# One Trainium2 core, expert blocks of a mixture-of-experts stage: which operand of the gate and up products is stationary

## The reference

```python
x = _layernorm(x + _L0_attn_ref(x, ...))   # latent attention, 16 heads
x = _layernorm(x + _L0_ffn_ref(x, gate_w, gate_up_proj, down_proj))
x = _layernorm(x + _L1_attn_ref(x, ...))   # 16 heads, 4 key groups
x = _layernorm(x + _L1_ffn_ref(x, weight, bias))
```

```python
gu = jnp.einsum('th,ehf->etf', x, gate_up_proj)     # h = 256, f = 2 * 128
gate, up = jnp.split(gu, 2, axis=-1)
inter = jax.nn.silu(gate) * up
y = jnp.einsum('eti,eih->eth', inter, down_proj)
out = jnp.einsum('eth,te->th', y, combine)          # combine: 0 but for 2 experts
```

## Time and profile before

| | |
|---|---|
| median of 3 executions | 537.47 us (536.35 to 539.25) |
| the profiled execution | 537.99 us |
| its span in the profile | 535.8 us |
| PE busy | 501.2 us |
| DVE, ACT, POOL busy | 377.3, 338.9, 294.7 us |
| expert stage, first turn_block to last POOL scatter | 225.6 to 281.3 us of the span |

### The profile page before, as it was taken

How to read it: one execution, slowest core, us unless ns; L and a number is a source line. 1 busy time by engine, 2 the same in 40 slices (tenths; PEclk the granted TensorE clock), 3 DMA queues, 4 the chain that set the end, 5 groups by cost and what they waited for, 6 DMA issues and landing times.

```text
span 535.8 us, 10729 instructions
## 1 busy us (share of the span) xinstructions
PE 501.2 (94%) x3600; PEld 437.3 (82%) x3600; DVE 377.3 (70%) x825; ACT 338.9 (63%) x755; POOL 294.7 (55%) x291
## 2 busy tenths in 40 slices
PE   7989999999999998799975879999999999999995
PEld 6768888888888787588854778999999999999884
DVE  2589888888885356755555788779766986678656
ACT  4457777777776655444432588778766876686673
POOL 4746777677775226336560577677544665465330
PEclk8999999999999999799996989999999999999999
DMA  8917999970000292345575000000000000000001
GB/s 265 393 64 281 323 314 329 332 252 0 0 0 1 94 410 79 105 132 160 166 256 187 1 1 2 0 1 2 1 1 2 0 1 2 1 2 1 1 21 60
DMA packets 17613, 56.79 MB, mean 106 GB/s; under 512 B 2612, under 2 KB 12346, under 8 KB 15770
## 3 DMA queue, kind: packets, MB, share of 16 engines
q1 hardware_dynamic: 14816, 49.81, 27.1%
q0 software_dynamic: 2752, 6.40, 3.6%
HBM read 49.19 MB, written 28.45 MB: 145 GB/s over the span
## 4 chain that ended last, share of the span: by engine, by line
PE 77%; DVE 8%; ACT 5%; issue 4%; POOL 3%; DMA 3%; SPq 0%; DVEq 0%; POOLq 0%; ACTq 0%
PE bank L442 10%; PE bank L444 10%; PE bank L443 10%; PE bank L990 5%; PE bank L585 5%; PE bank L507 5%; PE bank L610 3%; PE bank L587 2%; PE bank L734 2%; PE bank L1007 2%; PE bank L719 2%; PE bank L721 2%; PE bank L720 2%; PE bank L621 2%; PE bank L701 2%
## 5 line engine op out<-in xcount | busy, mean ns | idle before, releaser
L1099 ACT ACTIVATE probs<-bank,neg_max,q_scale 128x256 f32<-128x256 f32 (+1 forms) x128 | 63.8, 508 | 38.4 <-DVE neg_max L1742 38.4
L1951 POOL TENSOR_TENSOR probs<-probs,inv_sum 128x512 f32<-128x512 f32 x64 | 51.6, 828 | 44.3 <-DVE inv_sum L1750 44.3
L1984 POOL TENSOR_TENSOR exps<-exps,tables 128x256 f32<-128x256 f32 x32 | 24.6, 769 | 71.8 <-ACT exps L1209 71.7
L1209 ACT ACTIVATE exps<-bank 128x768 f32<-128x768 f32 x32 | 25.9, 809 | 41.3 <-PE bank L701 41.3
L1971 POOL TENSOR_TENSOR swapped<-swapped,tables 128x512 f32<-128x512 f32 x32 | 43.1, 1350 | 10.0 <-ACT swapped L1130 9.8
L1565 DVE TENSOR_TENSOR q_lo<-q_sum,q_hi 128x512 fp32r<-128x512 f32 x32 | 27.2, 851 | 29.7 <-ACT q_hi L1163 29.5
L2084 POOL DMA_INDIRECT y_rows<-y_slot,dest x31 | 29.7, 959 | 29.9 <-issue 19.1
L1728 DVE TENSOR_TENSOR swapped<-bank,tables 32x512 f32<-32x512 f32 x64 | 44.4, 694 | 1.4
L1943 POOL TENSOR_TENSOR qT<-qT,swapped 128x512 f32<-128x512 f32 x32 | 40.8, 1276 | 7.1 <-DVE swapped L1728 7.1
L442 PE MATMUL bank<-x,wq_hi 128*128 128x256 f32 x128 | 38.5, 301 | 3.2 <-DVE q_sum L1552 3.2
L585 PE MATMUL bank<-keysT,qT 128*128 128x256 f32 x128 | 38.3, 381 | 0.0
(11 more groups left out here) (283 smaller groups left out, 1774.2 us busy)
## 6 DMA issues: line engine op xcount, KB each, us to landing
slots<-in_c_unused SPq DMA_DIRECT2D x20, 1036.0 KB, 36.4
gu_all<-in_gate_up SPq DMA_DIRECT2D x4, 1024.0 KB, 7.9
xg<-slots SPq DMA_DIRECT2D x31, 129.5 KB
wvo_raw<-in_wvo SPq DMA_DIRECT2D x1, 2560.0 KB, 20.8
dn_all<-in_down SPq DMA_DIRECT2D x1, 2048.0 KB, 7.7
wq_full<-in_Wq SPq DMA_DIRECT2D x1, 2048.0 KB
wo_raw<-in_Wo SPq DMA_DIRECT2D x1, 2048.0 KB
wqk_raw<-in_wqk SPq DMA_DIRECT2D x1, 1536.0 KB, 10.4
```

The source lines that it names most:

```text
L1099: ins = act.activation(probs[:, par, h, c0:c1], bank[:, 2 * par + h, c0:c1], ACT.Exp, bias=neg_max[:, par, i:i + 1], scale=q_scale[:, b, t ...
L1951: ins = pool.tensor_tensor(some, some, inv, ALU.mult)
```

## The change

In `up` the weights become the stationary operand and the turned rows the moving one: four matmuls of 128 columns in place of two of 256, for gate and up apart. Their results have the 128 features of gate and up on partitions and the tokens along the free axis, which is the form that `down` needs, so DVE's product goes to `actT` directly; `turn_act`, `copy_act` and their PSUM banks are gone, and `down` follows `up` one step later instead of two. PE addresses a fixed place: a new ACT step, `take_weights(k)`, reads the expert's number with a `value_load` on ACT, waits for `up(k-2)` and copies the 512 columns of gate and up weights of block k to one of two buffers in `q_sum`. It stands behind `silu(k-2)` in ACT's order; the first two stand ahead of `copy_block(0)`. PE keeps its own `value_load`, for `down`. `up` has one wait more, on `gu_copied`.

```diff
--- before.py
+++ after.py
@@ -39,6 +39,7 @@
 W = D + 3
 KINDS = 8
 XG = 6
+GU = 2
 YS = 6
 WARM = (20, 42, 18, 14)
 ROUTE = 3 * E + PER_STEP + NB + NT
@@ -272,7 +273,8 @@
     eps, minus_half = table_probe[:, 19:20], table_probe[:, 17:19]
     idx_f = x_rows[:, :, D:D + TOP]
     xT_f32 = q_sum
-    gated, act_tok = (swapped[:, i, 0:2 * FF].rearrange("p (i n) -> p i n", i=2) for i in range(2))
+    gu_block = q_sum[:].rearrange("p g (c f) -> p g c f", c=KD)
+    gated = swapped[:, 0, 0:2 * P].rearrange("p (i n) -> p i n", i=2)
     wk_hi, wk_lo = w_hi, w_lo
     slots = nc.dram_tensor("slots", (REGIONS * REGION, W), F32, kind="Internal").ap()
     y_rows = nc.dram_tensor("y_rows", (TOP * (B * T + KINDS * REGION), D), F32, kind="Internal").ap()
@@ -299,7 +301,7 @@
 
     mo = sems("moe", "xT_copied region_ready row_ids logits_done sigmoid_done marked prefix_done slots_ready "
               "table_sums table_steps "
-              "xgT_done xgT_copied up_done silu_done act_ready actT_done actT_copied down_done y_copied dest_ready")
+              "xgT_done xgT_copied gu_copied up_done silu_done act_ready down_done y_copied dest_ready")
 
     kv = sems("kv1", "kv_hi kv_lo w_hi wq_lo w_lo k_done swap_done cos_done sin_done k_summed "
               "k_hi k_lo v_done v_copied ones")
@@ -378,9 +380,6 @@
 
     def up_bank(k):
         return 2 + k % 2
-
-    def actT_bank(k):
-        return 4 + k % 2
 
     def down_bank(k):
         return 6 + k % 2
@@ -980,26 +979,22 @@
                 mm = pe.transpose(bank[:, turned(k), c * P:c * P + P], xg[:, k % XG, c * P:c * P + P], ident[:])
             mm.then_inc(mo["xgT_done"], 1)
 
-        def up(k, experts):
+        def up(k):
             pe.wait_ge(mo["xgT_copied"], k + 1)
+            pe.wait_ge(mo["gu_copied"], k + 1)
             if k >= 2:
                 pe.wait_ge(mo["act_ready"], k - 1)
-            for c in range(KD):
-                for i, e in enumerate(experts):
-                    rows = slice(ROWS * i, ROWS * i + ROWS)
-                    mm = pe.matmul(bank[rows, up_bank(k), 0:2 * FF], xgT[:, k % 2, c, rows],
-                                   gu_all[:, bass.ds(e, 1), c, :].rearrange("p e f -> p (e f)"),
-                                   start=c == 0, stop=c == KD - 1, skip_group_check=True)
+            for i in range(PER_STEP):
+                rows = slice(ROWS * i, ROWS * i + ROWS)
+                for half in range(2):
+                    dst = bank[:, up_bank(k), half * P + ROWS * i:half * P + ROWS * i + ROWS]
+                    for c in range(KD):
+                        mm = pe.matmul(dst, gu_block[:, k % GU, c, half * FF:half * FF + FF], xgT[:, k % 2, c, rows], start=c == 0, stop=c == KD - 1,
+                                       skip_group_check=True)
             mm.then_inc(mo["up_done"], 1)
 
-        def turn_act(k):
+        def down(k, experts):
             pe.wait_ge(mo["act_ready"], k + 1)
-            if k >= 2:
-                pe.wait_ge(mo["actT_copied"], k - 1)
-            pe.transpose(bank[:, actT_bank(k), 0:P], act_tok[:, k % 2, :], ident[:]).then_inc(mo["actT_done"], 1)
-
-        def down(k, experts):
-            pe.wait_ge(mo["actT_copied"], k + 1)
             if k >= 2:
                 pe.wait_ge(mo["y_copied"], k - 1)
             for i, e in enumerate(experts):
@@ -1015,18 +1010,16 @@
             pe.wait_ge(x_or_expert_in[j], 32)
         turn_block(0)
         experts_of = {}
-        for i in range(STEPS + 2):
+        for i in range(STEPS + 1):
             if i < STEPS:
                 experts_of[i] = [pe.value_load(block_expert[0:1, m:m + 1], min_val=0, max_val=E - 1)
                                  for m in range(PER_STEP * i, PER_STEP * i + PER_STEP)]
             if i + 1 < STEPS:
                 turn_block(i + 1)
             if i < STEPS:
-                up(i, experts_of[i])
-            if 1 <= i <= STEPS:
-                turn_act(i - 1)
-            if i >= 2:
-                down(i - 2, experts_of.pop(i - 2))
+                up(i)
+            if i >= 1:
+                down(i - 1, experts_of.pop(i - 1))
 
         pe.wait_ge(mo["y_copied"], STEPS)
         pe.wait_ge(y_back[0], 16)
@@ -1341,21 +1334,35 @@
             act.activation(xgT[:, k % 2, :, :], bank[:, turned(k), 0:D].rearrange("p (c n) -> p c n", c=KD),
                            ACT.Copy).then_inc(mo["xgT_copied"], 1)
 
+        def take_weights(k):
+            e = act.value_load(block_expert[0:1, k:k + 1], min_val=0, max_val=E - 1)
+            if k >= GU:
+                act.wait_ge(mo["up_done"], k - GU + 1)
+            act.activation(gu_block[:, k % GU, :, :], gu_all[:, bass.ds(e, 1), :, :].rearrange("p e c f -> p (e c) f"),
+                           ACT.Copy).then_inc(mo["gu_copied"], 1)
+
         def silu(k):
             act.wait_ge(mo["up_done"], k + 1)
             if k >= 2:
                 act.wait_ge(mo["act_ready"], k - 1)
-            act.activation(gated[:, k % 2, :], bank[:, up_bank(k), 0:FF], ACT.Silu).then_inc(mo["silu_done"], 1)
+            act.activation(gated[:, k % 2, :], bank[:, up_bank(k), 0:P], ACT.Silu).then_inc(mo["silu_done"], 1)
 
         act.wait_ge(ld["wq1_in"], 16)
         act.wait_ge(ln["y_done"], NT)
         for i in range(PAIRS):
             act.activation(chunk(wq_hi, i), chunk(wq_full, i), ACT.Copy).then_inc(kv["w_hi"], 1)
+        act.wait_ge(mo["table_steps"], 4)
+        for j in range(4):
+            act.wait_ge(x_or_expert_in[j], 32)
+        take_weights(0)
+        take_weights(1)
         copy_block(0)
         for k in range(STEPS):
             if k + 1 < STEPS:
                 copy_block(k + 1)
             silu(k)
+            if k + 2 < STEPS:
+                take_weights(k + 2)
         load_table(act, 2 * B + 8, ACT.Sqrt)
         act_layer1(act)
 
@@ -1902,15 +1909,9 @@
         def gate_block(k):
             dve.wait_ge(mo["silu_done"], k + 1)
             if k >= 2:
-                dve.wait_ge(mo["actT_done"], k - 1)
-            dve.tensor_tensor(act_tok[:, k % 2, :], gated[:, k % 2, :], bank[:, up_bank(k), FF:2 * FF],
+                dve.wait_ge(mo["down_done"], k - 1)
+            dve.tensor_tensor(actT[:, k % 2, :], gated[:, k % 2, :], bank[:, up_bank(k), P:2 * P],
                               ALU.mult).then_inc(mo["act_ready"], 1)
-
-        def copy_act(k):
-            dve.wait_ge(mo["actT_done"], k + 1)
-            if k >= 2:
-                dve.wait_ge(mo["down_done"], k - 1)
-            dve.tensor_copy(actT[:, k % 2, :], bank[:, actT_bank(k), 0:P]).then_inc(mo["actT_copied"], 1)
 
         def copy_y(k):
             dve.wait_ge(mo["down_done"], k + 1)
@@ -1924,14 +1925,12 @@
                                      in1=xg[:, k % XG, D + 2:D + 3], op0=ALU.not_equal,
                                      op1=ALU.add).then_inc(mo["dest_ready"], 1)
 
-        for i in range(STEPS + 2):
-            if 1 <= i <= STEPS:
-                copy_act(i - 1)
+        for i in range(STEPS + 1):
             if i < STEPS:
                 gate_block(i)
                 find_rows(i)
-            if i >= 2:
-                copy_y(i - 2)
+            if i >= 1:
+                copy_y(i - 1)
         dve_layer1(dve, counted, n_step)
```

## The result

The changed kernel takes 534.68 us (median of 15 executions, 533.00 to 537.19), the kernel before, run beside it 15 times, 538.04 (536.28 to 543.22). The ratio is 0.9938 with a 95% interval from 0.9919 to 0.9958: 3.4 us less. The forecast was 534.2 us, with a range from 532.4 to 537.3.

The account below looks back on a forecast made before the run. The prediction took PE, busy throughout the expert stage, as the bound. Terms of -2.0, +0.1 and -1.4 gave -3.3 us: 534.7 from the profiled 537.99, and 534.2 for the median, 0.5 lower; range 532.4 to 537.3.

Parts of the forecast that it names:

- PE's step: Expert stage, PE's work per block: falls from 1.62 to 1.55 us, over 28 steps 2.0 us less.
- the rival with unhidden loads: PE in up: weight loads not hidden behind the products, step 2.41 us, 558 us in all; chance 0.02.
- ACT: Expert stage, ACT's added register load (0.7 us) and weights copy (0.52): hidden, with 1.1 us of work in a 1.55 us step.
- rival (a): ACT's register load takes 1.0 to 1.1 us, silu 0.2 to 0.3 late, step 1.60 to 1.63: 535.6 to 536.1; chance 0.24.
- the margin of 0.03 us: ACT's slack per step: silu can start 1.52 us after the previous silu's start and is due at 1.55.
- PE's register load: PE's expert-number load, now behind down: over at U+1.77, hidden with 0.2 us of cover, costed at nothing.
- U+1.97: Due time of the turn_block queued behind PE's expert-number load, 1.97 us after the end U of an up.
- The head: Pipeline fill at the expert stage's start: 0.1 us more, since down(0) now stands ahead of PE's expert-number load.
- rival (c): Granted clock: a stage ending 3 us sooner can gain or lose a low-clock stretch, up to 1.4 us; no separate chance.
- The margin of 1.4 us: Allowance on both sides of the forecast for a low-clock stretch gained or lost; forecast with it 532.6 to 535.8, chance 0.58.
- The end: Last up's end to last scatter's start: from 4.55 to 3.17 us, 1.38 less, with the last two scatters queued on POOL.
- The sum: Whole kernel: -2.0 + 0.1 - 1.4 = -3.3 us against the profiled execution of 537.99.

## Why the prediction was right

**PE's step.** Right to 0.01 us. up took 0.89 to 0.90, the step 1.546, and 28 of them gave -2.1 us where -2.0 stood. The price came from products of 129 columns with a new weight load each; the eight loads of up are hidden in the same way, and the rival with unhidden loads, 558 us, did not come. The Trainium skill ("TensorE: Matmul & The Clock Gate", Part 3, "What overlaps and what doesn't") asks for another row group for that; eight full-height loads and eight products in 0.90 us disagree with it.

**ACT.** Right, with less room than it looks. Silu to weights was 0.67 us (241.15 to 241.82), taken as 0.7; silu came 0.20 after up's end, as written; copy_block ended 1.76 us after it, where 1.80 stood. Silu follows copy_block without a gap, so the margin of 0.03 us that the sum left was about right. The run with two loads shows rival (a)'s side, the run with the weights copied once shows that nothing of it is paid in the changed kernel. That silu is late only by what exceeds the margin held where a load was added; that the pipeline can go uneven, with PE's ends reaching the others 1 to 2 us late, was in none of the cases. Here there was luck: the changed kernel happened to run in the even way, while two kernels with the same work on each engine, run on another chip, took 542.5 and 544.3, outside the range.

**PE's register load.** Right: turn_block came at 242.93, 1.98 us after up's end and without idle time, where U+1.97 stood; without the load the step is unchanged.

**The head.** Mis-sized: +0.1 stood there, +1.2 was measured in the profiled execution. It is rival (c)'s mechanism, a low-clock stretch in another place than before, not the new wait. The margin of 1.4 us that it had been given held it. In the medians, -3.4, this loss does not show.

**The end.** The last scatter began 3.29 us after the last up, not 3.17 (-1.3 for -1.4), and it is held by POOL's queue as said: the scatter before it went at 276.99 with 0.40 of issue, the last at 278.26, 1.27 later. The kernel with copies alone has 4.36 from the last silu, as before, and so has the turned product with down two steps behind (4.36, and 4.54 with even steps): the gain comes from down following up one step sooner, which the turned product allows.

**The sum.** -3.3 stood there. The profiled pair gives -2.7: 1.1 lost in the head, 0.4 gained outside the span, which had no term. The medians give -3.4.

## What to carry to other kernels

The transpose between two products was had for nothing here by exchanging which operand is stationary; price it by the records of a like product with a new load each, not by the number of loads. When a step is full on two engines, judge it by its steps one by one and not by their mean alone: uneven steps say that something else than the sum of work sets the time. When such a state exists, compare kernels only beside each other on one chip, and put one that is known to be even among them. Before moving a register load on ACT, look for the instruction ahead of it that still waits for a semaphore: the load began when that wait was over, so behind a long copy it was free (0.18 us from silu to the weights) and behind silu's wait it was not (0.67).

## What the runs showed of the hardware

- Register loads took longer where POOL's scatter started 0.1 to 0.2 us after them. In the kernel with down two steps behind up, PE's loads between 233 and 246 us took (min/median/max in ns; first and last start behind them):

```profile
L1015 PEldq TENSOR_LOAD <-block_expert x8: 297/557/602, 234.2 to 245.4; - x8
```

```profile
234.40 0.96 POOL L2083 DMA_INDIRECT y_rows<-y_slot,dest  x1 [0.58 <-issue]
```

 Over all traces of this case, PE's loads with a scatter 0.1 to 0.2 us behind them have a median of 0.55 us, the others 0.30; 14 of these 15 loads are of this one kernel. On ACT it is 0.45 (31 loads) against 0.28, and the two such loads in the kernel in which PE loads nothing took 0.53 at the middle, so it needs no load on PE. In the changed kernel the scatter comes 0.27 us after ACT's load and the load stays at its usual length:

```profile
L1338 ACTq TENSOR_LOAD <-block_expert x27: 272/301/430, 231.9 to 272.1; - x27
```

- The end of a product can reach the engines that wait for it, ACT and DVE, 1 to 2 us after its records say so, with PE's records running on. A timeline of PE alone shows such a step as full and healthy; the chain shows it as one product of 2.0 to 2.4 us. The cause is open.
- ACT's instruction stream has gaps of 0.3 us that belong to a place in the code: after silu 14 and 28 in the changed kernel, two steps earlier with the code shifted by 21 instructions, and 128 of ACT's records apart.
